# At most four scatters and eight gathers in flight, and four segments in the second aggregation

## The reference

```
x = x + L2norm(LN(x) @ w_self.T + segment_sum(w * LN(x)[src], dst) @ w_neigh.T)
x = x + shared_mlp(LN(x)) + top-2-of-4 experts(LN(x))            # "L0 ffn", dense
x = x + relu([LN(x), segment_sum(edge_attr, src) / max(count, 1), u] @ W1 + b1) @ W2 + b2
x = x + top-2-of-8 experts with 1024 hidden units(LN(x))         # "L1 ffn"
```

## Time and profile before

| | |
|---|---|
| median of three runs | 4248.87 us |
| the profiled execution | 4244.44 us, of which 4242.7 us are the span |
| PE busy | 2596.5 us (61%) |
| POOL busy | 1886.1 us (44%) |
| DVE busy | 1421.7 us (34%) |
| ACT busy | 974.0 us (23%) |
| mean granted clock of PE | 0.785 |
| gathers, L340 | 784, 69.0 to 1265 us |
| scatters, L353 and L901 | 784, 1265.3 to 2351 us |
| last store of the dense layers, L976 | 2864.8 us |
| second aggregation on PE, L1174 | 2884.6 to about 3200 us |

### The profile page before, as it was taken

One profiled execution on the slowest core, in us unless ns is written; L12 is line 12 of the kernel. 1 busy time (PEld: TensorE's weight loads), 2 busy tenths in 40 slices (PEclk: granted clock), 3 DMA queues, 4 the chain that ended last, 5 costly groups with the idle time before them and its releaser, 6 DMA issues. The chain is left out here.

```text
span 4242.7 us, 48077 instructions
## 1 busy us (share of the span) xinstructions
PE 2596.5 (61%) x11859; PEld 1995.8 (47%) x11860; DVE 1421.7 (34%) x3597; ACT 974.0 (23%) x2337; POOL 1886.1 (44%) x1901
## 2 busy tenths in 40 slices
PE   0445545555562122011111699998999879999998
PEld 0333334334452001010000366657996668888898
DVE  5221225666521000000000244438995542222222
ACT  4555322222220000000000244430003421111122
POOL 4566655665666777777777100002000342222222
PEclk9776666777776555555555799999998889999999
DMA  6223323232222111111111000005553454444455
GB/s 188 81 85 91 91 83 95 87 89 81 85 86 64 53 53 51 42 51 51 61 42 42 22 18 18 35 18 171 146 146 116 162 152 110 112 115 118 106 147 149
DMA packets 217916, 372.79 MB, mean 88 GB/s; under 512 B 48901, under 2 KB 146542, under 8 KB 216815
## 3 DMA queue, kind: packets, MB, share of 16 engines
q0 software_dynamic: 82928, 157.51, 14.1%
q1 hardware_dynamic: 77100, 154.03, 10.9%
q10 hardware_dynamic: 57812, 60.35, 4.8%
HBM read 290.03 MB, written 81.71 MB: 88 GB/s over the span
## 5 line engine op out<-in xcount | busy, mean ns | idle before, releaser
L670 PE MATMUL psum<-arena 128*128 x1984 | 633.1, 482 | 524.0 <-issue 277.8
L340 POOL DMA_INDIRECT arena<-xn_rows,arena x784 | 747.0, 953 | 453.8 <-issue 241.3
L901 POOL DMA_INDIRECT sorted_edges<-arena x768 | 796.1, 1037 | 252.4 <-issue 252.1
L670 PEld LDWEIGHTS psum<-arena 128*128 128x128 f32 x1984 | 463.4, 244 | 693.7 <-issue 616.8
L405 ACT ACTIVATE arena<-arena 128x256 f32<-128x256 f32 x784 | 338.0, 496 | 691.8 <-DMA arena<-xn_rows,arena 619.5
L1174 PE MATMUL psum<-arena,acc 128*65 128x128 f32 x2720 | 311.8, 275 | 23.7 <-DVE arena L1327 23.7
L1100 PE MATMUL psum<-arena 128*128 128x512 f32 (+1 forms) x336 | 167.9, 654 | 249.4 <-issue 167.9
L1174 PEld LDWEIGHTS psum<-arena,acc 128*65 128x65 f32 x2720 | 295.8, 138 | 40.0 <-DVE arena L1327 31.9
L1793 PE MATMUL psum<-arena,xr 128*128 x1344 | 302.8, 383 | 12.1 <-DVE xr L2018 5.3
L1780 PE MATMUL psum<-xr 128*128 128x256 f32 x1344 | 299.6, 381 | 1.0 <-DVE xr L2012 1.0
L572 DVE TENSOR_TENSOR acc<-acc,psum 128x256 f32 x248 | 102.9, 415 | 541.8 <-remote 395.0
(11 more groups left out here) (310 smaller groups left out, 3155.1 us busy)
## 6 DMA issues: line engine op xcount, KB each, us to landing
xr<-in_f_W_dram SPq DMA_DIRECT2D x63, 1024.0 KB
acc<-sorted_edges ACTq DMA_DIRECT2D x340, 132.0 KB, 2.1
arena<-in_attr_dram SPq DMA_DIRECT2D x28, 924.0 KB
arena<-xn_rows,arena POOLq DMA_INDIRECT x784
sorted_edges<-arena POOLq DMA_INDIRECT x784
arena<-hidden_parts SPq DMA_DIRECT2D x7, 1792.0 KB, 7.1
arena<-dispatched SPq DMA_DIRECT2D x42, 265.0 KB
arena<-in_f_W_dram SPq DMA_DIRECT2D x8, 1024.0 KB
```

The source lines that it names most:

```text
L340: pool.indirect_dma_start(out=rows[:, c, :], out_offset=None, in_=xn_d, in_offset=bass.IndirectOffsetOnAxis(ap=idx[:, c:c + 1], axis=0)).t ...
L670: last = nc.tensor.matmul(psum[:, bank(u), 0:D], hot[:, u, c, :], rows[:, ds(slots[k] + c, 1), :].squeeze(1), start=c == 0, stop=c == RUN - 1)
L901: pool.indirect_dma_start(out=edges_d, out_offset=bass.IndirectOffsetOnAxis(ap=pos_i[:, c:c + 1], axis=0), in_=stage[:, q % 2, c % SC, :], ...
```

## The change

Four things are altered.

1. EACH goes from 4 to 2, so the scatters go in batches of two. Before batch b POOL waits that batch b-2 has landed, so no more than four scatters are in flight, where there could be eight. BEGUN stays 16.
2. In the gather loop POOL waits, before the four gathers of a slot, until the gathers of the slot two before it have landed (`s_gat[(u - 2) % SLOTS]`). So no more than eight gathers are in flight, where up to 28 could be.
3. The segments of the counting sort and of the second aggregation are 532, 156, 56 and 40 columns instead of 448, 224 and 112.
4. An assertion is shortened.

```diff
-SEGMENTS = ((0, 448), (448, 672), (672, NC))
+SEGMENTS = ((0, 532), (532, 688), (688, 744), (744, NC))
...
-EACH = 4
+EACH = 2
...
-BEGUN = 4 * EACH
-assert QUARTERS == 4 and QUARTERS * SC * NG == NC and 4 * SC // EACH == 28
+BEGUN = 16
+assert QUARTERS == 4 and QUARTERS * SC * NG == NC
...
                             if u in (0, IDX_PARTS[1]):
                                 pool.wait_ge(s_idx, it * 2 + (u > 0) + 1)
+                                alone(pool)
+                            if u >= 2 or not first:
+                                pool.wait_ge(s_gat[(u - 2) % SLOTS], it * (16 * RUN) + (16 * RUN if u >= 2 else 0))
                                 alone(pool)
```

## The result

The changed kernel takes 4302.6 us (median of four runs, 4290.56 to 4309.3) against 4248.74 us (median of four, 4238.77 to 4254.17). The ratio is 1.0118, with a 95% interval of 1.0102 to 1.0135. It is slower by 54 us, 1.2%, clear of the interval. The forecast was 3345 us; rival (a), "everything stays but 48 items", had said 4298.

A forecast was written before the change was run, and what follows sets the result against it. Bound: PE idles about 940 us because the scatter stream delays its signals. Gathers end 1154, dense layers 1854, scatters 2215, stage 3 2296; plus 1044 gives 3340, with 4.4 for the median 3345 us; range 3240 to 3500.

The forecast's parts named there:

- rival (a): Scatters: the stream itself causes the stall, new limits may never bind; all stays but 48 items, 4298 us; chance 0.20.
- the backlog of signals: Scatters: every indirect DMA adds to a backlog that other engines' signals pass through; begins after some ten us, drains in 20.
- Part 1: Scatters in batches of two: POOL stops when signals back up, PE runs dense layers beside scatters at 1.33 us each.
- the 651 us of the dense layers: Dense layers beside the scatters: 592 us of work at the later pace plus 10% for remaining interference.
- The argument on the backlog: Scatters: the backlog of 1047 us drained in 20, so holding the stream down by about 2% should cost POOL little.
- Part 2: Gather loop: 194 added waits cost nothing and relieve late signals, so the gathers end at 1154 instead of 1265 us.
- The relief of 110 us: Gather loop: of 210 us that POOL waits for products, only 100 were taken to remain.
- Part 3: New segments: 48 more items in stage 3 cost 44.6 us; the last segment waits for 40 columns' scatters instead of 112.
- Nothing for stage 1: Ranking beside the gathers: the fourth scan's 10 us of DVE cost nothing, since POOL sets the pace there.
- the forecast's own route: Stage 3: dense layers come free, so it starts at 1874 us, catches up with the scatters and ends at 2296.
- the port nor the DMA sharing: Stage 3 beside scatters: if items slow well above 0.93 us, one was mis-sized; DMA shares sum to 0.68, so both fit.
- The frame of the sum: Whole kernel: dense layers start 49 us after the gathers, stage 3 ends behind the last scatter, then 1044 us follow unchanged.

The follow-up runs named there:

- e3: The kernel before, but POOL waits for the end of the dense layers before the 768 scatters of the second block: 4283.6 us in its one run.
- e9: The kernel before with scatter batches of one (EACH = 1), so at most two scatters are in flight: 4243.0 us.
- e4: The kernel before, but before every fourth scatter of the second block POOL waits for all earlier ones to land: 3738.6 us in its one run.

## Why the prediction was wrong

**What bounds the kernel.** Right: e3 shows that the scatter stream and nothing of PE's own stalls the dense layers, with 791 matmuls in 200 us once it is absent. By what route the scatters hold PE's signals up stays open, and with it the backlog of signals that the prediction supposed. For every execution on record there is a recorded clock, so every one was recorded by the profiler; whether the stall is there without the recording, no run shows.

**Part 1, the step that failed.** "The loop is closed by the very signals that are late: if they back up, POOL stops until they come." The scatters' landings are seldom late; what PE hands over is. In the changed kernel 12 gaps in 767 are put down to a landing, in e9 with two in flight 73. So the loop did not close: the stream took 1048.8 us instead of 1047.0, and 1.367 us a scatter where the sum had 1.33. The term of the sum that fell with it is the 651 us of the dense layers. From the first scatter of the second block at 1321.8 to their last store at 2885.9 there are 1564 us. The prediction had the contrary evidence in the earlier trace rows, no wait for a landing with the old limit, used it to price the wait at nothing, and put it under rival (a) with 0.20 instead of drawing the conclusion: a wait that costs nothing because it hardly ever binds cannot relieve anything either. The cost of the wait (nothing) and its benefit (a pause) are the same number.

**The argument on the backlog.** "The stream is over the limit by no more than about 2%" had no ground. The tail of 20 to 24 us behind the last scatter is there before and after, but what cleared the stall were pauses of 1.5 to 2 us that add 14% (runs of twelve) to 35% (runs of four) to the spacing of 1.27 us; the mean spacing of before, 1.365, already has 7% of them. What the tail is remains open.

**Part 2.** The waits in the gathers cost nothing, as said. The relief of 110 us was wrong for the same reason: they never bind.

**Part 3.** 44.6 us for 48 items was right to 0.3 us. Nothing for stage 1 was wrong: it named 10 and 7 us as the cost if DVE became the bound there, and the last gather starts 17.2 us later in the changed kernel and 13.7 with the segments alone. That DVE is the bound there was not tested. Rival (a) had the mechanism, the limits hardly bind. Its 4298 against 4302.6 owes something to luck, a partial cancellation of 63 us of segments and 16 from the limits.

**Stage 3 beside scatters.** The sum took 0.929 us an item there. With pauses that free the dense layers it is 1.78 us at runs of eight and 1.05 at four; by the forecast's own route (PE free, stage 3 behind the scatters) the new segments would still not have paid. Neither the port nor the DMA sharing that the prediction's last sentence names shows: DVE's one-hots kept their 744 to 747 ns in every run, and items were slower at a DMA share of 0.44 (runs of eight) than at 0.62 (runs of four).

**The frame of the sum** held where it could be tried. e4 starts its dense layers at about 1305 and ends them at 1915, 610 us against 651 taken; stage 3's last addition followed the last scatter by 86 us; what comes behind took 3738.6 - 2698.6 = 1040 us against 1044.

## What to carry to other kernels

If a wait is meant to hold a stream back, look first whether it would ever have ended an idle time: a limit that the stream hardly reaches changed nothing here, a drain did. Where one engine's long stream of small indirect DMAs stands beside others that idle on "remote", break the stream: a pause of about 2 us after every four to eight gave 12 to 15% here. Do not price a pipeline stage that newly stands beside such a stream by the pace it has alone, and time what lies near an edge on more than one chip.

## What was not expected of the hardware

- An unbroken stream of POOL's indirect scatters (0.97 us each, one per 1.27 us) holds what PE hands over by ten us, though the DMA share is 0.16. With runs of 4 and pauses of 1.5 to 2 us it does not (787 matmuls in 200 us), and with 8 hardly in the dense layers; with 16 it does for most of the time (136 matmuls in 200 us).
- Indirect DMAs of POOL do it and other work of POOL does not: 1690 memsets in 570 us left PE busy 560. Other kinds of DMA from POOL were not tried.
- A lower limit in flight does not help: with at most two (4243 us) and at most eight (4249) it is alike, and even two was seldom reached.
- PE's clock follows: 0.54 in the stalled stretch, 0.98 with runs of four.
- One kernel near the edge took 3601.7 us on one chip and 3695.6 on another ten minutes later, where the kernel before took 4247.4 and 4268.2.
